# Turned attention weights sent from SBUF to SBUF in 16 transfers per pair of heads, their buffers doubled, and the projection weights placed where expert parameters come later

## The chip, the cores and the metric

One core of one Trainium2 chip runs the whole layer in one launch. The metric is the device time of one execution in microseconds (us), the median over runs. The profile is of one other execution of the same program; its times are read within that execution.

## The reference

The input is x, 8 batches of 512 tokens of width 128, float32. Two blocks follow each other, each with a layer norm ahead and a residual around it:

```
q, k, v = split_heads(ln(x) @ Wq), ...          # 16 heads of 64
scores  = q @ k^T + bias(rel_bias)              # 32 buckets of relative position
x       = x + (softmax(scores) @ v merged) @ Wo
h       = ln(x)
logits  = -|h - keys|^2 + h @ rw^T + rb          # 16 experts
w, e    = softmax(top4(logits))
x       = x + sum_k w_k * (gelu(h @ w1[e_k]^T + b1[e_k]) @ w2[e_k]^T + b2[e_k])
```

## The kernel before

**Attention.** The outer loop runs over the 8 batches b, the inner one over 8 pairs of heads i (`run_steps`); n = 8b + i numbers the pairs, 0 to 63. A step of TensorE computes the scores of its pair in four row tiles v (L1334) for the two heads hh, projects v, q and k for the next pair (L1285 to L1287), and finishes the pair before: it turns the probabilities of the row tiles v = 2, 3 with TensorE (`weights_t`, L1348) and multiplies them by the values in `weigh_late` (L1387); `weigh_early` (L1403) does the same for the row tiles v = 0, 1 and is the last thing in the step. The product with Wo follows a step later (`project_out`, L1414). All is float32; the projections and scores are made of three products of high and low parts.

Between score and product, VectorE adds the bias and finds the row maximum (L1040), ScalarE takes the exponential (L884), VectorE the reciprocal of the sum (L1046), and GpSimd divides (L816).

**How the row tiles v = 0, 1 are turned.** `turn_blocks` (VectorE, L1062) transposes blocks of 32 x 32 of `prob` into `turned`, two transposes for each v; they are counted in `tr_rdy`, four to a pair. The blocks then still have to move across groups of 32 partitions, which VectorE can't do. SP does it in `turn_weights`: for each v it stores `turned` into `pt_dram` in four transfers of 32 partitions each (128 KB, L678), and once all have landed loads the v half of `pt_d` from there in one transfer of 512 KB (L686). There is one `turned` and one `pt_d`. VectorE may write `turned[:, v]` for a pair only when the stores of the pair before have landed (`pt_wr[v]`), and SP may load `pt_d` only when `weigh_early` of the pair before is done (`c_rdy`). `weigh_early` waits for `pt_rd`. The very first pair and the last one (63) go by TensorE transposes and VectorE copies instead.

**SP's order.** SP issues everything in the order in which it is written in `step(b, i)`: `turn_weights` of the pair, at times the load of a batch of x, then expert parameters. Each expert is two transfers (`load_expert`, 514 KB and 64 KB, L655 and L656) into `params`, which overlaps the front of `shared` (AHEAD columns that nothing else uses) and then the bias `strips`, which come free pair by pair in the last batch. Five experts are loaded in batches 1 to 5, the other eleven in the last batch, the last two of them (`last_experts`) between the two halves of the stores of pair 62. `first_rows` fetches the first three blocks of gathered rows (`xb`, L734) between the two loads of that pair.

**Expert blocks.** After attention 79 blocks of 256 gathered rows follow, each for one expert: rows turned (L1469), hidden layer (L1481 to L1483), GELU (L916), second layer (L1494), result scattered (L851). In the last attention step, and in `drain`, the first blocks are interleaved with the end of attention: `turn(0, 0)` stands directly ahead of `weigh_early` of pair 62 on TensorE.

**Memory.** `w_hi`, `w_lo` (high and low parts of the three projection weights) belong to attention; `xb`, the gathered rows, takes memory that attention has given up, so `first_rows` waits for the last projection.

Of the kernel before, what the change touches and what calls it, by code (L numbers as in the profile page):

```python
# [20 lines left out]
F32 = mybir.dt.float32  # L21
# [8 lines left out]
P = 128  # L30
DH = 64
# [6 lines left out]
def layer_kernel(nc, x, wq, wk, wv, wo, rel_bias, onehot, ident, expert_no, before_tok, region, home_row, pad,  # L38
# [47 lines left out]
    with ExitStack() as ctx:  # L86
# [79 lines left out]
        turned = sb("turned", [P, 2, TC, TC, 2, BK], stack=attn)  # L166
        pt_d = sb("pt_d", [P, 2, TC, TC, 2, BK], stack=attn)
# [4 lines left out]
        stage = [turned[:, n].rearrange("p k j h r -> p (k j h r)") for n in range(2)]  # L172
        stage.append(pt_e[:].rearrange("p h j q -> p (h j q)")[:, 0:H * DH])
        scratch = shared[:, AHEAD + H * STRIP:]
# [7 lines left out]
        pt_dram = nc.dram_tensor("pt_dram", [2, 2, P, TC, TC * 2 * BK], F32, kind="Internal").ap()  # L182
# [24 lines left out]
        tr_rdy, pt_wr, pt_rd = sem("tr_rdy"), [sem(f"pt_wr{v}") for v in range(2)], [sem(f"pt_rd{v}") for v in range(2)]  # L207
# [14 lines left out]
        attn.close()  # L222

        xbt_hi = sb("xbt_hi", [P, 2, BLK], F32R)
# [3 lines left out]
        xb = sb("xb", [P, UN, BC, D + 1])  # L228
        home = sb("home", [P, UN, BC], I32)
        act_h = sb("act_h", [P, 2, FC, BLK])  # L230
# [6 lines left out]
        yk = shared[:, NE * EW:NE * EW + YB * TOP * S].rearrange("p (a k c d) -> p a k c d", k=TOP, c=TC, d=D)  # L237
# [19 lines left out]
        FIRST, OTHERS = slice(0, VW), slice(VW, H * DH)  # L257
# [380 lines left out]
        def _(sp):  # L638
# [31 lines left out]
            def turn_weights(b, i):  # L670

                n = b * NPR + i
                for v in range(2):
                    sp.wait_ge(tr_rdy, 4 * n + 2 * v + 2)
                    if n >= 3:
                        sp.wait_ge(pt_rd[v], 16 * (n - 2))
# [3 lines left out]
                    if v == 0 and (b, i) == (LAST, NPR - 2):  # L680
                        last_experts()
# [1008 lines left out]
```

## Time and profile before

| | us |
|---|---|
| median of 3 runs | 1121.62 (1121.6 to 1124.82) |
| profiled execution, first to last instruction | 1087.2 |
| TensorE busy | 1056.9 (97%) |
| VectorE busy | 834.8 (77%) |
| ScalarE busy | 839.7 (77%) |
| GpSimd busy | 685.9 (63%) |

The DMA engines moved 189.09 MB, and HBM was read for 101.18 MB and written for 88.23 MB. The attention steps last to about 765 us, the expert blocks from about 787 us to the end. A time is in microseconds from the first instruction; "busy" of TensorE counts matmuls, whose ends are modelled. In a row of the waits, the engine and line that waited stand ahead of the arrow, and what it waited for behind it. The hardware queue of SP is called SPq, its rows are the issues of transfers; when a transfer lands is another matter, told by the chain of waits or by the section on DMA.

### The profile page before, as it was taken

How to read it: one execution, taken by the hardware profiler on the slowest of the kernel's cores; microseconds unless marked ns; L12 is line 12 of the kernel's file. 1: busy time of each engine (PE TensorE's matmuls, PEld its weight loads, DVE VectorE, ACT ScalarE, POOL GpSimd, SP SyncE). 2: the span in 40 equal slices, each digit the busy share in tenths (PEclk: the TensorE clock that was granted, in tenths of full speed). 3: DMA queues.
4: the chain of work that ended last, by engine and by line, in shares of the span. 5: the costliest groups of instructions: out<-in, count | busy, mean ns of one | idle time of the engine just before them, and what ended most of it. 6: DMA issues, size and time to landing. Idle time of an engine off the chain costs nothing.

```text
span 1087.2 us, 27487 instructions
## 1 busy us (share of the span) xinstructions
PE 1056.9 (97%) x8509; PEld 863.7 (79%) x8510; DVE 834.8 (77%) x2568; ACT 839.7 (77%) x2050; POOL 685.9 (63%) x890
## 2 busy tenths in 40 slices
PE   8999999999999999999999999999799999999993
PEld 4777777777777777777777777777599999999993
DVE  6877888888888978988898888888546444457775
ACT  5888888888888888888888888878667666777661
POOL 4654556774776568477657756665756777655553
PEclk9999999999999999999999999999999999999997
DMA  7676666776676677576757666787722623234552
GB/s 212 177 198 192 194 172 181 206 210 171 207 208 184 179 198 208 165 222 194 201 163 216 194 174 194 207 261 227 252 66 82 158 70 105 79 95 133 162 174 69
DMA packets 135344, 189.09 MB, mean 174 GB/s; under 512 B 19000, under 2 KB 108608, under 8 KB 135216
## 3 DMA queue, kind: packets, MB, share of 16 engines
q1 hardware_dynamic: 126064, 170.65, 55.5%
q0 software_dynamic: 9152, 16.88, 4.6%
q8 instruction: 63, 1.03, 0.4%
q14 instruction: 65, 0.53, 0.2%
HBM read 101.18 MB, written 88.23 MB: 174 GB/s over the span
## 4 chain that ended last, share of the span: by engine, by line
PE 80%; DMA 6%; DVE 5%; issue 4%; POOL 2%; SPq 1%; ACT 1%; DVEq 0%; POOLq 0%; ACTq 0%
PE bank L1334 14%; PE bank L1494 13%; PE bank L1403 9%; PE bank L1348 8%; PE bank L1387 8%; PE bank L1414 4%; PE bank L1481 3%; PE bank L1483 3%; PE bank L1482 3%; PE bank L1285 3%; PE bank L1287 3%; PE bank L1286 3%; DMA pt_d<-pt_dram 3%; DVE shared L1040 2%; DMA pt_dram<-turned 2%
## 5 line engine op out<-in xcount | busy, mean ns | idle before, releaser
L816 POOL TENSOR_SCALAR shared<-shared,rinv 128x512 f32<-128x512 f32 x512 | 351.8, 699 | 224.9 <-DVE rinv L1046 222.9
L884 ACT ACTIVATE shared<-shared,nmax 128x512 f32<-128x512 f32 x512 | 368.4, 733 | 75.8 <-DVE nmax L1040 75.8
L1040 DVE CUSTOM_DVE_ANT_0 shared<-bank,shared 128x512 f32<-128x512 f32 x512 | 330.1, 682 | 77.6 <-issue 33.1
L851 POOL DMA_INDIRECT y_dram<-yb,home x158 | 162.0, 1026 | 94.0 <-issue 47.6
L372 POOL DMA_INDIRECT xs_dram<-copies,slot x128 | 134.8, 1053 | 62.0 <-issue 48.9
L1062 DVE STREAM_TRANSPOSE turned<-shared 128x512 f32<-128x512 f32 x248 | 161.0, 687 | 10.7 <-issue 10.7
L890 ACT ACTIVATE pt_e<-bank 128x512 f32<-128x512 f32 x256 | 145.1, 596 | 18.0 <-PE bank L1348 17.2
L1494 PE MATMUL bank<-shared,act_h 128*128 x1264 | 154.1, 275 | 1.3 <-DVE yb L1188 0.7
L1494 PEld LDWEIGHTS bank<-shared,act_h 128*128 128x128 f32 x1264 | 148.0, 192 | 1.9 <-issue 1.9
L1348 PE MATMUL bank<-idn,shared 128*128 128x128 f32 x1024 | 136.6, 276 | 0.5 <-DVE nmax L1040 0.5
L1348 PEld LDWEIGHTS bank<-idn,shared 128*128 128x128 f32 x1024 | 112.8, 141 | 24.1 <-issue 12.7
L1387 PE MATMUL bank<-pt_e,v_sb 128*64 128x256 f32 x1024 | 124.6, 385 | 3.5 <-DVE nmax L1040 3.0
L916 ACT ACTIVATE act_h<-bank,shared 128x256 f32<-128x256 f32 x316 | 124.2, 476 | 3.4 <-PE bank L1483 3.2
L1403 PE MATMUL bank<-pt_d,v_sb 128*64 128x256 f32 x1008 | 122.7, 385 | 3.8 <-DMA pt_d<-pt_dram 3.5
L1387 PEld LDWEIGHTS bank<-pt_e,v_sb 128*64 128x64 f32 x1024 | 71.1, 136 | 49.2 <-issue 23.6
L1334 PE MATMUL bank<-k_hi,q_lo 64*128 64x512 f32 x512 | 109.1, 421 | 0.9 <-DVE q_lo L1023 0.6
L884 ACT ACTIVATION_READ_ACCUMULATOR shared<-shared,nmax 128x1 f32 x512 | 106.6, 208 | 0.0
L1403 PEld LDWEIGHTS bank<-pt_d,v_sb 128*64 128x64 f32 x1008 | 73.6, 138 | 38.3 <-issue 7.9
L1334 PE MATMUL bank<-k_hi,q_hi 64*128 64x512 f32 x512 | 101.0, 388 | 0.0
L1334 PE MATMUL bank<-k_lo,q_hi 64*128 64x512 f32 x512 | 100.9, 388 | 0.0
L1481 PE MATMUL bank<-xbt_hi,w_lo 128*128 128x256 f32 x316 | 95.6, 303 | 0.0
L1188 DVE TENSOR_TENSOR yb<-bank,shared 128x256 f32<-128x256 f32 x79 | 33.5, 424 | 79.9 <-PE bank L1494 79.9
(162 smaller groups left out, 1886.7 us busy)
## 6 DMA issues: line engine op xcount, KB each, us to landing
pt_dram<-turned SPq DMA_DIRECT2D x496, 128.0 KB
pt_d<-pt_dram SPq DMA_DIRECT2D x124, 512.0 KB
xb<-xs_dram SPq DMA_DIRECT2D x79, 129.0 KB, 2.9
shared<-in_experts SPq DMA_DIRECT2D x16, 514.0 KB
shared<-y_dram SPq DMA_DIRECT2D x32, 256.0 KB, 4.6
shared<-roll_dram SPq DMA_DIRECT2D x4, 768.0 KB, 8.2
y_dram<-yb,home POOLq DMA_INDIRECT x158
xs_dram<-pad_sb SPq DMA_DIRECT2D x17, 129.0 KB, 2.2
```

The lines of the kernel that those rows point to most:

```text
L372: pool.indirect_dma_start(xs_dram, bass.IndirectOffsetOnAxis(ap=slot[:, c * TOP + k:c * TOP + k + 1], axis=0), copies[:, c, k % 2, :], Non ...
L816: pool.tensor_scalar(tile, tile, rinv[:, 2 * v + hh:2 * v + hh + 1], 1.0, ALU.mult, ALU.mult)\
L851: pool.indirect_dma_start(y_dram, bass.IndirectOffsetOnAxis(ap=home[:, j, c:c + 1], axis=0), yb[:, j, c, :], None, bounds_check=last_row, ...
L884: act.activation(prob[:, v, hh, :], prob[:, v, hh, :], ACT.Exp, bias=nmax[:, n:n + 1], scale=-1.0, accum_out=rsum[:, n:n + 1]).then_inc(ex ...
L890: act.activation(pt_e[:, hh, :, (v - 2) * P:(v - 1) * P], weights_bank(b, i, v, hh)[:].rearrange("p (j q) -> p j q", j=TC), ACT.Copy)\
L1040: dve.tensor_tensor_reduce(prob[:, v, hh, :], score_bank(v, hh)[:], strips[:, 2 * i + hh, v * P:v * P + S], -1.0, BIG, ALU.add, ALU.min, n ...
L1062: dve.transpose(turned[:, v, :, :, hh, :].rearrange("p k j r -> p j k r"), prob[:, v, hh, :].rearrange("p (j k c) -> p j k c", k=TC, c=BK) ...
L1334: mm = pe.matmul(score_bank(v, hh)[:], q[rows, i % 2, v * P:(v + 1) * P], k[rows, i % 2, :], start=(m == 0), stop=(m == 2))
L1348: mm = pe.transpose(weights_bank(b, i, v, hh)[:, j * P:(j + 1) * P], prob[:, v, hh, j * P:(j + 1) * P], idn[:])
L1387: pe.matmul(ps_a[DH * hh:DH * hh + DH, 2 * P:4 * P], v_sb[:, i // 2 % 2, j, col:col + DH], pt_e[:, hh, j, :], start=(j == 0), stop=(j == T ...
L1403: mm = pe.matmul(ps_a[DH * hh:DH * hh + DH, 0:2 * P], v_sb[:, i // 2 % 2, j, col:col + DH], src[:, :, :, j, hh, :].rearrange("p v a r -> p ...
L1494: mm = pe.matmul(ps_y[:, c * D:(c + 1) * D], act_h[:, q % 2, f, c * P:(c + 1) * P], params[:, bass.ds(w + (W2 + f * D), D)], start=(f == 0 ...
```

## The change

`turned` and `pt_d` get a second buffer each, chosen by the parity of the pair. `pt_dram` goes. SP waits for all four transposes of a pair and for `weigh_early` of two pairs before, and then issues 16 transfers, one for each group of 32 source partitions a and each group of 32 target partitions k: 32 partitions, two runs of 1 KB in each, 64 KB in all. They count up `pt_sent` of the parity, on which `weigh_early` waits; VectorE waits on it too, for the pair two before, ahead of the transposes.

To make room, the high and low projection weights become one tensor `weights`, laid out pair by pair at the front of the memory that `params` takes later, so that it comes free pair by pair in the last batch. `free_at(e, i)` says whether expert e fits into what is free after step i, and all 16 experts are loaded in the last batch, in the steps 0 to 6: experts 0; 6, 7; 1, 8; 2, 9, 10; 11, 12; 3, 13; 4, 5, 14, 15. Those of step 6 are issued ahead of `turn_weights` of pair 62, and `first_rows` behind it. `xb` gets memory of its own for the whole kernel.

```diff
@@ -139,39 +139,40 @@
+        xb = sb("xb", [P, UN, BC, D + 1])
 
 
         PROBS = 2 * TC * S
-        AHEAD = max(0, NE * EW - (H - 2) * STRIP)
-        shared = sb("shared", [P, AHEAD + H * STRIP + PROBS])
-        strips = shared[:, AHEAD:AHEAD + H * STRIP].rearrange("p (h m) -> p h m", h=H)
-        prob = shared[:, AHEAD + H * STRIP:].rearrange("p (c h s) -> p c h s", c=TC, h=2)
-        params = shared[:, 0:NE * EW]
+        AHEAD = NPR * 6 * P
+        assert NE * EW <= AHEAD + (H - 2) * STRIP
+        low = ctx.enter_context(ExitStack())
+        weights = sb("weights", [P, NPR, 3, 2, P], F32R, low)
+        shared = sb("shared", [P, H * STRIP + PROBS], stack=low)
+        strips = shared[:, 0:H * STRIP].rearrange("p (h m) -> p h m", h=H)
+        prob = shared[:, H * STRIP:].rearrange("p (c h s) -> p c h s", c=TC, h=2)
...
-        w_hi = [sb(f"w{n}_hi", [P, H * DH], F32R, attn)[:] for n in "kqv"]
-        w_lo = [sb(f"w{n}_lo", [P, H * DH], F32R, attn)[:] for n in "kqv"]
...
+        pt_d = sb("pt_d", [P, 2, 2, TC, TC, 2, BK], stack=attn)
...
-        turned = sb("turned", [P, 2, TC, TC, 2, BK], stack=attn)
-        pt_d = sb("pt_d", [P, 2, TC, TC, 2, BK], stack=attn)
+        turned = sb("turned", [P, 2, 2, TC, TC, 2, BK], stack=attn)
...
+        low.close()
+
+        late = sb("late", [P, AHEAD + H * STRIP + PROBS])
+        params = late[:, 0:NE * EW]
...
+        FIRST, OTHERS = slice(0, 2), slice(2, NPR)
+        PIECES = TC * TC * 16
+
+        def sent_by(n):
+
+            return PIECES * ((n + 1) // 2)
...
             def turn_weights(b, i):
 
                 n = b * NPR + i
-                for v in range(2):
-                    sp.wait_ge(tr_rdy, 4 * n + 2 * v + 2)
-                    if n >= 3:
-                        sp.wait_ge(pt_rd[v], 16 * (n - 2))
-                    for a in range(TC):
-                        sp.dma_start(pt_dram[n % 2, v].rearrange("(k c) a e -> a c k e", k=TC)[a],
-                                     turned[a * BK:(a + 1) * BK, v].rearrange("c k j h r -> c k (j h r)")).then_inc(pt_wr[v], 16)
-                    if v == 0 and (b, i) == (LAST, NPR - 2):
-                        last_experts()
-                if n:
-                    sp.wait_ge(c_rdy, n)
-                for v in range(2):
-                    sp.wait_ge(pt_wr[v], 64 * n)
-                    sp.dma_start(pt_d[:, v].rearrange("p a j h r -> p (a j h r)"),
-                                 pt_dram[n % 2, v].rearrange("p a e -> p (a e)")).then_inc(pt_rd[v], 16)
-                    if v == 0 and (b, i) == (LAST, NPR - 2):
-                        first_rows()
-
-            def free_to(b, i):
-
-                return AHEAD if b < LAST else AHEAD + 2 * STRIP * (i + 1)
-
-            loaded = [0]
-
-            def last_experts():
-
-                sp.wait_ge(neg_rdy, LAST * CHUNKS + (NPR - 1) * TILES)
-                while loaded[0] < NE:
-                    load_expert(loaded[0])
-                    loaded[0] += 1
+                par = n % 2
+                sp.wait_ge(tr_rdy, 4 * n + 4)
+                if n >= 2:
+                    sp.wait_ge(c_rdy, n - 1)
+                for a in range(TC):
+                    for k in range(TC):
+                        sp.dma_start(pt_d[k * BK:(k + 1) * BK, par, :, a].rearrange("c v j h r -> c v (j h r)"),
+                                     turned[a * BK:(a + 1) * BK, par, :, k].rearrange("c v j h r -> c v (j h r)"))\
+                            .then_inc(pt_sent[par], 16)
+
+            def free_at(e, i):
+
+                first, end = e * EW, (e + 1) * EW
+                used_up = (i + 2) // 2 * 2 * 6 * P + i % 2 * 4 * P
+                return (first >= AHEAD or min(end, AHEAD) <= used_up) and (end <= AHEAD or end <= AHEAD + 2 * STRIP * (i + 1))
+
+            def experts_of(i):
+
+                return [e for e in range(NE) if free_at(e, i) and not (i and free_at(e, i - 1))]
+
+            def load_experts(i):
+
+                sp.wait_ge(k_rdy, LAST * NPR + min(i + 2, NPR))
+                sp.wait_ge(neg_rdy, LAST * CHUNKS + (i + 1) * TILES)
+                for e in experts_of(i):
+                    load_expert(e)
 
             def load_table():
 
...
             def step(b, i):
+                if (b, i) == (LAST, NPR - 2):
+                    load_experts(i)
                 if (b, i) not in ((0, 0), (LAST, NPR - 1)):
                     turn_weights(b, i)
+                if (b, i) == (LAST, NPR - 2):
+                    first_rows()
                 n = b * NPR + i + 1
                 if 2 <= n < NB:
                     sp.dma_start(x_all[:, n * TC:(n + 1) * TC, :],
                                  x[n * S:(n + 1) * S].rearrange("(n p) d -> p n d", p=P)).then_inc(ld_x, 16)
-                if b == LAST:
-                    sp.wait_ge(neg_rdy, LAST * CHUNKS + (i + 1) * TILES)
-                for _ in range(2 if b == LAST else 1 if 1 <= b < 6 and i == 6 else 0):
-                    if loaded[0] < NE and (loaded[0] + 1) * EW <= free_to(b, i):
-                        load_expert(loaded[0])
-                        loaded[0] += 1
+                if b == LAST and i < NPR - 2:
+                    load_experts(i)
 
             run_steps(step, lambda: None)
-            assert loaded[0] == NE
+            assert sum(len(experts_of(i)) for i in range(NPR - 1)) == NE
             run_blocks(sp, block_rows, lambda: None, LEAD - 1, rows, row_at, rest, looped=FETCH_FROM // UN)
             for n in range(LATE_STORES, NB):
                 store(n)
...
                 if (b, i) == (0, 0):
                     copy_first(v)
                     return
-                if later_turn(b, i):
-                    dve.wait_ge(pt_wr[v], 64 * (b * NPR + i - 1))
+                n = b * NPR + i
+                if n > 2:
+                    dve.wait_ge(pt_sent[n % 2], sent_by(n - 2))
                 for hh in range(2):
                     dve.wait_ge(norm_rdy, b * CHUNKS + TILES * i + 2 * v + hh + 1)
                     if hh == 0:
                         dve.nop(nofuse=True)
-                    dve.transpose(turned[:, v, :, :, hh, :].rearrange("p k j r -> p j k r"),
+                    dve.transpose(turned[:, n % 2, v, :, :, hh, :].rearrange("p k j r -> p j k r"),
                                   prob[:, v, hh, :].rearrange("p (j k c) -> p j k c", k=TC, c=BK)).then_inc(tr_rdy, 1)
 
             def copy_early(v):
 
                 n = LAST * NPR + NPR - 1
-                dve.wait_ge(pt_wr[v], 64 * (n - 1))
+                dve.wait_ge(pt_sent[n % 2], sent_by(n - 2))
                 for hh in range(2):
                     dve.wait_ge(early_rdy, 2 * v + hh + 1)
                     if hh == 0:
                         dve.nop(nofuse=True)
-                    dve.tensor_copy(turned[:, v, :, :, hh, :].rearrange("p a j r -> p j a r"),
+                    dve.tensor_copy(turned[:, n % 2, v, :, :, hh, :].rearrange("p a j r -> p j a r"),
                                     early_bank(v, hh)[:].rearrange("p (j a r) -> p j a r", j=TC, a=TC)).then_inc(tr_rdy, 1)
 
             def copy_first(v):
...
                 n = b * NPR + i
                 last = n == NB * NPR - 1
                 src = turned if last else pt_d
+                par = n % 2
                 if last or n == 0:
                     pe.wait_ge(tr_rdy, 4 * (n + 1))
                 else:
-                    for v in range(2):
-                        pe.wait_ge(pt_rd[v], 16 * n)
+                    pe.wait_ge(pt_sent[par], sent_by(n))
                 for j in range(TC):
                     for hh in range(2):
                         col = (i % 2) * P + DH * hh
                         mm = pe.matmul(ps_a[DH * hh:DH * hh + DH, 0:2 * P], v_sb[:, i // 2 % 2, j, col:col + DH],
-                                       src[:, :, :, j, hh, :].rearrange("p v a r -> p (v a) r"),
+                                       src[:, par, :, :, j, hh, :].rearrange("p v a r -> p (v a) r"),
                                        start=(j == 0), stop=(j == TC - 1))
                 mm.then_inc(c_rdy, 1)
 
```

The engines' code for the projections and for `weights_hi` and `weights_lo` names the same columns in `weights`, and `copy_early` and `copy_first` name the buffer of their parity.

## Rows read from the trace of the kernel before

**Rows 1.** The page, busy time of each engine, share of the span, instructions.

```profile
PE 1056.9 (97%) x8509; PEld 863.7 (79%) x8510; DVE 834.8 (77%) x2568; ACT 839.7 (77%) x2050; POOL 685.9 (63%) x890
```

**Rows 2.** Windows: length, busy time of each engine, granted clock, DMA share, GB/s.

```profile
95.00:760.00 665.00, 662.15 (x5263) 504.83 (x5260) 571.30 (x1811) 552.62 (x1350) 429.40 (x588) 1.00 0.69 197
760.00:800.00 40.00, 33.80 (x261) 26.15 (x261) 17.80 (x49) 25.77 (x63) 26.68 (x34) 0.96 0.56 187
```

**Rows 3.** Waits of TensorE before `weigh_early`: total us, times, longest us.

```profile
PE bank L1403 <- DMA pt_d<-pt_dram: 3.5, 5, 1.7
PEld bank L1403 <- issue: 7.9, 12, 2.0
```

**Rows 4.** Timeline of VectorE, the later transposes of pairs 16, 19 and 21.

```profile
213.93 1.29 DVE L1062 STREAM_TRANSPOSE turned<-shared 128x512 f32<-128x512 f32 x2
...
247.99 0.70 DVE L1062 STREAM_TRANSPOSE turned<-shared 128x512 f32<-128x512 f32 x1
...
274.57 0.71 DVE L1062 STREAM_TRANSPOSE turned<-shared 128x512 f32<-128x512 f32 x1 [1.22 <-issue]
```

**Rows 5.** Timeline of TensorE, the first `weigh_early` matmuls of the same three pairs.

```profile
224.52 0.39 PE L1403 MATMUL bank<-pt_d,v_sb 128*64 128x256 f32 x2
...
261.31 0.44 PE L1403 MATMUL bank<-pt_d,v_sb 128*64 128x256 f32 x2
...
285.13 0.44 PE L1403 MATMUL bank<-pt_d,v_sb 128*64 128x256 f32 x2
```

**Rows 6.** Chain of waits from 570 to 586 (pair 46): start, us, what.

```profile
575.02 0.44 SPq L678
575.46 0.04 issue
575.50 2.54 DMA pt_dram<-turned
...
578.05 6.64 DMA pt_d<-pt_dram
584.69 0.14 issue
```

**Rows 7.** Timeline of SP's queue, two bursts of four issues.

```profile
215.25 1.75 SPq L678 DMA_DIRECT2D pt_dram<-turned  x4
...
429.93 2.15 SPq L678 DMA_DIRECT2D pt_dram<-turned  x4
```

**Rows 8.** The page's DMA issues: the one store of 64 KB, us to landing.

```profile
roll_dram<-shared SPq DMA_DIRECT2D x1, 64.0 KB, 1.9
```

**Rows 9.** Windows with columns as in rows 2: four stores, and the junction's start.

```profile
215.90:217.90 2.00, 2.00 (x19) 1.40 (x16) 1.97 (x7) 1.24 (x3) 1.83 (x3) 1.00 0.84 214
...
764.00:774.00 10.00, 9.05 (x78) 7.17 (x79) 7.80 (x24) 6.65 (x18) 8.58 (x11) 1.00 0.91 320
```

**Rows 10.** DMA queue of instructions: packets, MB, share; whole span, and 429.7 to 431.2.

```profile
q8 instruction: 63, 1.03, 0.4%
...
q8 instruction: 1, 0.02, 4.1%
```

**Rows 11.** All issues of line 678: duration ns min/median/max, first and last start.

```profile
L678 SPq DMA_DIRECT2D pt_dram<-turned x496: 302/436/1745, 32.0 to 771.6; - x166
```

**Rows 12.** Timeline of SP's queue at the junction.

```profile
767.13 0.82 SPq L656 DMA_DIRECT2D shared<-in_b  x1
...
772.26 0.96 SPq L686 DMA_DIRECT2D pt_d<-pt_dram  x1
774.42 1.55 SPq L734 DMA_DIRECT2D xb<-xs_dram  x3
778.95 0.33 SPq L686 DMA_DIRECT2D pt_d<-pt_dram  x1
```

**Rows 13.** Timeline of TensorE at the junction.

```profile
780.91 0.41 PE L1469 MATMUL bank<-idn,xb 128*128 128x128 f32 x2 [0.91 <-DMA xb<-xs_dram]
783.06 3.63 PE L1403 MATMUL bank<-pt_d,v_sb 128*64 128x256 f32 x16 [1.74 <-DMA pt_d<-pt_dram]
```

More of the change, by code:

```diff
@@ L165, in layer_kernel @@
         rinv = sb("rinv", [P, TILES], stack=attn)
-        turned = sb("turned", [P, 2, TC, TC, 2, BK], stack=attn)
-        pt_d = sb("pt_d", [P, 2, TC, TC, 2, BK], stack=attn)
+        turned = sb("turned", [P, 2, 2, TC, TC, 2, BK], stack=attn)
         pt_e = sb("pt_e", [P, 2, TC, 2 * P], stack=attn)
         ctxt = sb("ctxt", [P, S], stack=attn)
-        stage = [turned[:, n].rearrange("p k j h r -> p (k j h r)") for n in range(2)]
+        stage = [turned[:, 0, n].rearrange("p k j h r -> p (k j h r)") for n in range(2)]
         stage.append(pt_e[:].rearrange("p h j q -> p (h j q)")[:, 0:H * DH])
-        scratch = shared[:, AHEAD + H * STRIP:]
+        scratch = shared[:, H * STRIP:]
         onehot_sb = scratch[0:NBUCKET, 0:ROLL].rearrange("p (a m) -> p a m", a=2)
@@ L206, in layer_kernel @@
         early_rdy, first_rdy = sem("early_rdy"), sem("first_rdy")
-        tr_rdy, pt_wr, pt_rd = sem("tr_rdy"), [sem(f"pt_wr{v}") for v in range(2)], [sem(f"pt_rd{v}") for v in range(2)]
+        tr_rdy, pt_sent = sem("tr_rdy"), [sem("pt_sent_even"), sem("pt_sent_odd")]
         c_rdy, c_cp, o_rdy, res_rdy = (sem(n) for n in ("c_rdy", "c_cp", "o_rdy", "res_rdy"))
@@ L234, in layer_kernel @@
         pad_at = sb("pad_at", [1, NE], I32)
-        yk = shared[:, NE * EW:NE * EW + YB * TOP * S].rearrange("p (a k c d) -> p a k c d", k=TOP, c=TC, d=D)
+        yk = late[:, NE * EW:NE * EW + YB * TOP * S].rearrange("p (a k c d) -> p a k c d", k=TOP, c=TC, d=D)
         ps_xt, ps_y, ps_h = banks[0], banks[1], (banks[2:4], banks[4:6])
@@ L984, in weights_hi @@
             def weights_hi(n, cols):
-                act.activation(w_hi[n][:, cols], stage[n][:, cols], ACT.Copy).then_inc(w_hi_rdy, 1)
+                act.activation(weights[:, cols, n, 0], stage[n].rearrange("p (i c) -> p i c", c=P)[:, cols], ACT.Copy).then_inc(w_hi_rdy, 1)
             act.wait_ge(ld_w[0], 16)
@@ L1106, in weights_lo @@
                 dve.wait_ge(w_hi_rdy, order)
-                dve.tensor_tensor(w_lo[n][:, cols], stage[n][:, cols], w_hi[n][:, cols].bitcast(F32), ALU.subtract)\
+                dve.tensor_tensor(weights[:, cols, n, 1], stage[n].rearrange("p (i c) -> p i c", c=P)[:, cols],
+                                  weights[:, cols, n, 0].bitcast(F32), ALU.subtract)\
                     .then_inc(w_lo_rdy, 1)
@@ L1289, in project_k @@
             def project_k(i, bank):
[L1291 to L1292 removed]
+                three(bank[:], weights[:, i, 0, 0], weights[:, i, 0, 1], xnt_hi[:], xnt_lo[:]).then_inc(k_rdy, 1)
             def project_q(i, bank):
[L1296 to L1297 removed]
+                three(bank[:], weights[:, i, 1, 0], weights[:, i, 1, 1], xnt_hi[:, ::-1], xnt_lo[:, ::-1]).then_inc(q_rdy, 1)
             def project_v(i, bank):
[L1301 removed]
+                pairs = slice(i // 2 * 2, i // 2 * 2 + 2)
                 for a in range(2):
@@ L1304, in project_v @@
                     tok = slice(c * P, (c + 1) * P)
-                    mm = three(bank[:, a * VW:(a + 1) * VW], xnt_hi[:, tok], xnt_lo[:, tok],
-                               w_hi[2][:, cols], w_lo[2][:, cols])
+                    mm = three(bank[:, a * VW:(a + 1) * VW].rearrange("p (i c) -> p i c", c=P), xnt_hi[:, tok], xnt_lo[:, tok],
+                               weights[:, pairs, 2, 0], weights[:, pairs, 2, 1])
                 mm.then_inc(v_rdy, 1)
```

14 lines of the change are left out of this document (2 added, 12 removed).

## The prediction

> **What bounds the kernel now.** I read the page's busy line first [rows 1]: TensorE is busy for 1056.9 of 1087.2 us, so only about 30 us can be won from waits. The windows say where they lie [rows 2]: in the attention steps between 95 and 760 us TensorE is busy for 662.15 of 665 us, so 2.85 us are idle; in the 40 us in which attention gives way to the expert blocks 6.2 us are idle, and the mean clock is 0.96, which costs 40 x 0.04 = 1.6 us more. The waits name what I can win [rows 3]: `weigh_early` (L1403) waited 3.5 us for the transfer into `pt_d`, in five places, and its weight loads 7.9 us in twelve (these views count the same waits twice and include start-up of the pipeline). The other 30-odd us are the start, the tail and the junction's waits for VectorE, which the change doesn't touch.
>
> So the question is narrow: when do the turned weights of a pair arrive, against the time at which TensorE comes to them? Call A the time from the end of a pair's last transpose to the start of its `weigh_early` in an undelayed step. Pair 16: 213.93 + 1.29 = 215.22 to 224.52, A = 9.30. With the same 1.29 for two transposes, pair 21 has 275.86 to 285.13, A = 9.27, and pair 19 has 249.28 to 261.31, A = 12.0 [rows 4, 5]. A depends on the place in a batch of eight pairs. Pairs 21 and 19 are the ends of the eight; read the same way, places 0, 4 and 5 lie at 9.30, 9.5 and 9.27, places 1, 6 and 7 at about 9.9, places 2 and 3 at 11 and 12.
>
> Before, the way goes through DRAM [rows 6]: the last of four stores starts at 575.50 and is seen done 2.54 us later, the read that follows lands after another 6.64 us, TensorE starts 0.14 us after that. This pair (46) was late by some 0.4 to 0.8 us. An ordinary pair arrives 1 to 2 us early: margins are thin already.
>
> **The change, part by part.** The eight stores and two loads of a pair become 16 SBUF-to-SBUF transfers of 64 KB, issued only when all four transposes are done.
>
> Call R the time from the last transpose to data ready. Issue: four back-to-back issues take 1.75 us [rows 7], and one of them repeats every 0.44 + 0.04 = 0.48 us [rows 6], so the first takes 1.75 - 3 x 0.48 + 0.04 = 0.35. The last of 16 thus starts 0.02 + 0.35 + 14 x 0.48 = 7.1 us after the transpose. I assume that the issue costs the same for a quarter of a store's pieces; no row shows a form like it. Landing of the last: no row shows an SBUF-to-SBUF transfer. The nearest are the one 64 KB store out of SBUF, 1.9 us [rows 8], and the last store of a burst of four with the others queued before it, 2.54. Below these it may lie, since nothing goes to DRAM and nothing is queued: in 215.9 to 217.9 the four stores flow at 214 GB/s [rows 9], at which 64 KB take 0.31 us, less than the 0.48 between issues, so no backlog forms. I take 1.8, nearest to the 1.9 row, with 1.2 and 2.54 as ends. R = 7.1 + 1.8 + 0.14 = 9.0; ends 8.4 and 9.8.
>
> At 9.0 no place waits. But the chain of 16 issues is exposed to disturbances. Instruction packets of 16 KB (63 in 1087 us, one in 17 us) pass through the same DMA engines, and the burst beside one took 2.15 instead of 1.75 us [rows 7, 10]; the longest single issue is 1.745 against 0.436 [rows 11]. Issue and landing last 9 us, so about half of the pairs meet one; I take +0.7 us, between 0.4 and the 1.3 of the longest. Then R = 9.7 and places 5, 0 and 4 wait 0.45, 0.40 and 0.2. A wait at one pair is slack for the next, which hardly matters here. Sum: 1.05 a batch, x 0.5, x 62 / 8 = 4 us added. Against this stand the waits of before between 95 and 760, which go whole: -3 us.
>
> The doubled buffers: SP's new wait for `c_rdy` is for `weigh_early` two pairs back (done by 1.9 us after its start, a step before), and VectorE's for `pt_sent` of two pairs back, 23 us old at the transpose. Both are over long before, so nothing queued behind them on SP (the load of `x_all`, the experts) or on VectorE is held. DRAM loses 124 MB of traffic (62 pairs, 1 MB each way); nothing in attention waits for bandwidth. The layout of `weights` and the own place of `xb` cost nothing: the same instructions with other strides, on ScalarE and VectorE, which are not late, and `first_rows` keeps its waits.
>
> Expert parameters: all 16 now come in the last batch (before, 11), by `free_at` in steps 0 to 6: 1, 2, 2, 3, 2, 2, 4. Each is two issues, 0.95 us of SP. In step 3 that is 2.9 us after 7.6 us of turning, 10.5 of an 11.5 us step: it fits.
>
> The junction: before, SP issued two experts between the two halves of pair 62's stores, the first load of `pt_d` at 772.26 (0.96 us), the first rows of `xb` at 774.42, and the second load only at 778.95, when the stores had landed behind the experts [rows 12]. TensorE turned `xb` at 780.91 and started `weigh_early` at 783.06, 1.74 us idle, then at half clock [rows 13]. After: SP is through with pair 61 and its two experts at about 766, four experts take 8 x 0.48 = 3.8, to 770; 16 transfers take 7.6, to 777.6; their data stand behind some 3.5 MB of experts, which at the 320 GB/s of this stretch [rows 9] need 11 us and are gone by 776, so they land at 779.5. `first_rows` comes last: 1.2 us of register loads as between 773.2 and 774.4, issue at 779, landing 2.1 to 2.9 us later, 781.5. `turn(0, 0)` stands ahead of `weigh_early` on TensorE, so this starts at 781.6 to 782 instead of 783.06: -1.5 us at most, +1.5 if the queue of experts holds SP back (such issues took up to 0.8 us [rows 12]). I take -1.
>
> Sum: -3 + 4 - 1 = 0, rounded to -1 for the gain at the junction's clock, of which 1.6 us is the bound. The profiled execution would go from 1087.2 to about 1086; the median of the runs shown is 1121.6, 34.4 above that span, and none of this lies in the edits. So 1120.5.
>
> A rule against the change: the Trainium skill, "DMA: Bandwidth & Descriptors", section "Rules for kernel authors", says to coalesce many small transfers, since under 64 KB one pays mostly overhead. The traces hold overheads apart from each other: four issues in 1.75 us, landing 2.54 us after the last. By the rule's section on one DMA, a fixed 2.0 us each, 16 in a row would be an estimated 32 us a pair; by that row they overlap, and only the last one's counts.
>
> **The rivals.**
> 1. Faster. The last transfer lands in 1.2 us, R = 8.4, 9.1 with a disturbance: no place ever waits. -3, the junction at -3 because the rows come sooner too, and its 1.6 us of clock: -7.6, 1114. For it: SBUF is both ends, no backlog. Against it: the 1.9 us row.
> 2. Slower: the issue chain takes the place of the round trip. From R = 9.27 on, undisturbed pairs wait. With 2.54 for the landing R = 9.8: places 4, 5 and 0 wait 0.3, 0.25 and 0.5, 1.0 a batch; disturbed (10.5) the places 4, 5, 6, 7, 0 wait 1.0, 0.25, 0.4, 0.15, 1.0, 2.8 in all. The mean 1.9 x 62 / 8 = 15 us, -3 and -1: +11, 1132. For it: every 0.1 us of the issue interval is 1.4 us of R.
> 3. The transfers don't flow. 32 partitions give 214 GB/s where four stores do it together [rows 9]; if an SBUF-to-SBUF piece goes at half of that, it takes 0.61 us, 16 x 0.61 + 1.6 = 11.4: waits of 1.9, 0.25, 1.3, 0.2, 1.9 and 0.4 in places 4 to 7, 0 and 2 (each wait takes something off the next), 5.9 a batch, 46 us; net +42, 1163. The Trainium skill ("SBUF — State Buffer", "Door 1: The DMA port swizzle") says that 32 partitions reach 8 of the 16 ports, an estimated 218 GB/s of its 436; the row's 214 agrees for stores. Against the rival: reads and writes have never shared a burst here.
>
> **How the numbers follow.** Forecast 0.42, rival 1 0.27, rival 2 0.25, rival 3 0.06. A difference under 0.3% (3.4 us) can't be told from none; the forecast's own range is 1117.5 to 1124.5, the other cases lie outside. So faster 0.27, same 0.42, slower 0.31. The range takes in rivals 1 and 2 with some way beyond the second's 1132, and leaves out rival 3 and the far ends: 1113 to 1138.
>
> **What would show it.** In the profile after: the first to the last of 16 issues 7.1 us, more in about half of the pairs; the last one landing 1.2 to 2.5 us on; waits of `weigh_early` of about 4 us in places 0, 4 and 5 of the batches, none in 2 and 3; SP's issues of experts at 766 to 770 and `weigh_early` of pair 62 near 782. The prediction is wrong if an issue of this form takes other than 0.44 us, if waits appear in places 2 and 3 (rival 3), or if SP stops between issues because the DMA engines are full.

## The result and the profile after

The changed kernel is slower: 1226.2 us median against 1121.61 us, ratio 1.0911 (95% interval 1.0885 to 1.0937). The experiments below ran later, on three chips, on which the kernel before took 1087.54, 1088.25 and 1088.15 us; once more there, the changed kernel has 1193.17 against 1088.25 us, ratio 1.098 (1.0939 to 1.1022). So both kernels were some 33 us quicker than in the first comparison, and the loss in microseconds is the same, 104.6 and 104.9. Each ratio is to the kernel before on the same chip.

The page of the first profile after, busy time as in [rows 1] and the HBM line; then the waits, columns as in [rows 3]:

```profile
PE 1104.1 (90%) x8509; PEld 879.7 (72%) x8510; DVE 830.6 (68%) x2568; ACT 839.8 (69%) x2050; POOL 692.5 (57%) x890
...
HBM read 36.16 MB, written 23.22 MB: 49 GB/s over the span
```

```profile
PEld bank L1403 <- DMA pt_d<-turned: 83.9, 40, 4.0
...
PE bank L1403 <- DMA pt_d<-turned: 69.7, 36, 3.5
```

TensorE, 97% busy before, is busy for 90% of a span of 1223.8 us. `weigh_early` (L1403) waits 69.7 us for the transfers where it waited 3.5 us. The DRAM traffic is gone as intended, and it gained nothing.

Why it waits is seen in one pair. The chain of waits of the changed kernel, pair 22, columns as in [rows 6]; 11 of the 16 issues are left out, and the last one is the start of the row of the DMA:

```profile
319.79 1.22 DVE turned L1066 x2
321.01 0.02 issue
321.02 0.59 SPq L686
321.61 0.04 issue
321.65 0.60 SPq L686
...
324.86 1.10 SPq L686
...
330.47 0.60 SPq L686
331.07 0.04 issue
331.11 2.06 DMA pt_d<-turned
333.18 0.04 issue
333.22 1.95 PE bank L1403 x16
```

An issue repeats every 0.60 + 0.04 = 0.64 us, not every 0.48 as those of [rows 6]. The last of 16 starts at 331.11, 10.1 us after the transposes (9.6 us had none been held up; one took 1.10 us). It has landed 2.06 us later, and TensorE starts at 333.22: R = 12.2 us, above every A of [rows 4, 5]. All issues of the form, columns as in [rows 11]:

```profile
L686 SPq DMA_DIRECT2D pt_d<-turned x992: 585/597/1917, 37.3 to 879.3; - x199
```

The median is 597 ns against 436 for the stores, and the shortest, 585 ns, is close to it: no issue of this form is cheap. The long ones have company: each of the 36 issues above 0.9 us overlaps one of the 62 packets of 16 KB of instructions, as in [rows 10], while only 66 of all 992 issues do.

### The profile page after: what moved, and what is told of

It reads as the page before. It is cut to its first block, busy times and chain, and to the rows that moved or that the text cites. A ratio compares the mean times of both kernels' runs of the same rounds, so it can differ in the third digit from the quotient of the medians.

```text
span 1223.8 us, 27682 instructions
## 1 busy us (share of the span) xinstructions
PE 1104.1 (90%) x8509; PEld 879.7 (72%) x8510; DVE 830.6 (68%) x2568; ACT 839.8 (69%) x2050; POOL 692.5 (57%) x890
## 4 chain that ended last, share of the span: by engine, by line
PE 37%; SPq 25%; DVE 17%; issue 7%; DMA 7%; ACT 3%; POOL 2%; another core or an unknown queue 0%; ACTq 0%; DVEq 0%; POOLq 0%
SPq L686 24%; PE bank L1494 13%; PE bank L1403 7%; DVE shared L1043 6%; PE bank L1334 6%; DMA pt_d<-turned 5%; DVE turned L1066 4%; PE bank L1483 3%; PE bank L1481 2%; PE bank L1482 2%; DVE q_lo L1026 1%; POOL shared L819 1%; DVE k_lo L1021 1%; PE bank L1469 1%; PE bank L1348 1%
## 5 line engine op out<-in xcount | busy, mean ns | idle before, releaser
L854 POOL DMA_INDIRECT y_dram<-yb,home x158 | 169.8, 1075 | 128.6 <-issue 81.7
L1403 PE MATMUL bank<-pt_d,v_sb 128*64 128x256 f32 x1008 | 145.9, 440 | 69.7 <-DMA pt_d<-turned 69.7
L1494 PE MATMUL bank<-late,act_h 128*128 x1264 | 161.9, 283 | 10.8 <-ACT act_h L919 5.7
L1403 PEld LDWEIGHTS bank<-pt_d,v_sb 128*64 128x64 f32 x1008 | 78.5, 156 | 123.0 <-DMA pt_d<-turned 83.9
L1494 PEld LDWEIGHTS bank<-late,act_h 128*128 128x128 f32 x1264 | 151.9, 196 | 17.6 <-issue 17.4
L919 ACT ACTIVATE act_h<-bank,late 128x256 f32<-128x256 f32 x316 | 125.4, 480 | 42.4 <-remote 22.5
L900 ACT ACTIVATE ctxt<-bank 128x512 f32<-128x512 f32 x64 | 38.4, 600 | 134.6 <-PE bank L1403 124.2
L1190 DVE TENSOR_TENSOR yb<-bank,late 128x256 f32<-128x256 f32 x79 | 33.5, 424 | 111.5 <-PE bank L1494 83.2
```

Of the source, the lines that this page charges most:

```text
L854: pool.indirect_dma_start(y_dram, bass.IndirectOffsetOnAxis(ap=home[:, j, c:c + 1], axis=0), yb[:, j, c, :], None, bounds_check=last_row, ...
L1403: mm = pe.matmul(ps_a[DH * hh:DH * hh + DH, 0:2 * P], v_sb[:, i // 2 % 2, j, col:col + DH], src[:, par, :, :, j, hh, :].rearrange("p v a r ...
L1494: mm = pe.matmul(ps_y[:, c * D:(c + 1) * D], act_h[:, q % 2, f, c * P:(c + 1) * P], params[:, bass.ds(w + (W2 + f * D), D)], start=(f == 0 ...
```

## The experiments

Theory A: SP's chain of issues, 16 at 0.64 us behind the last transpose, makes the weights late; the stalls, and half clock behind them, are the loss. Rival B: the rest of the change (memory layout, experts in the last batch, `first_rows` behind everything) costs a good part. Rival C: the transfers' data flow is slow between 32 partitions, not their issue. The expectations of the first four runs count absolute times from the 1121.6 us of the first comparison; what compares is the ratio.

### The kernel before and the kernel after, once more

> The kernel before, once more, for its span and the way its time is spread. The profiled execution of before had a span of 1087.2 us beside a median of 1121.6, that of the changed kernel 1223.8 beside 1226.2. If the profiled execution of before was merely a quick one, this one's span lies near 1119 us and the 32 us more lie in the expert blocks (blocks of 3.5 to 4 us instead of 3.44), not in attention, whose steps stay at 11.5 to 13.2 us.

Measured: 1086.39 us, ratio 0.9997 (0.9981 to 1.0013), span 1085.9. The profile of before shown above, with its span of 1087.2, is like the executions here and unlike the 1121.6 us beside it; the span near 1119 did not come. The medians on the three chips lie within 0.8 us of each other, so the first comparison's 1121.6 stands alone; whether its chip or something else of that occasion made it so, no run shows.

> The changed kernel once more, beside the kernel before on this chip, for a comparison inside one chip of attention (95 to 750 us) and the expert blocks. Theory A: a ratio of 1.085 to 1.095 to before; all of it in attention and at the junction, 85 to 100 us: 60 to 70 us of waits of weigh_early and 1.7 us for each stretch of half clock that follows one; the expert blocks as before within 3 us. Rival B': part of the loss lies in the expert blocks (the first profile of after had 35 us more there than that of before), because something of the change slows them: then 20 us or more in the blocks here too.

Measured: 1193.17 us, ratio 1.098, span 1189.0; ratio and loss are a little above what I expected. Windows, columns as in [rows 2], from the first instruction to the start of `weigh_early` of pair 62, so that both hold the same work, and from there to the end: first of before, then of after.

```profile
0.00:782.90 782.90, 770.01 (x6036) 582.02 (x6038) 660.66 (x2073) 643.96 (x1568) 492.79 (x699) 1.00 0.70 200
782.90:1085.90 303.00, 284.62 (x2474) 280.86 (x2474) 174.61 (x496) 194.88 (x482) 190.81 (x192) 0.98 0.37 108
```

```profile
0.00:885.40 885.40, 798.91 (x6035) 589.89 (x6036) 660.15 (x2071) 643.83 (x1567) 499.91 (x707) 0.96 0.43 103
885.40:1189.00 303.60, 286.07 (x2475) 281.23 (x2474) 174.87 (x497) 194.87 (x483) 184.30 (x184) 0.97 0.38 109
```

Nearly all of the loss lies ahead of that point: 885.4 against 782.9, 102.5 us more. The expert blocks take 303.6 against 303.0, so rival B' falls. The 102.5 us split into two terms. TensorE's idle time grew from 12.9 (782.9 - 770.01) to 86.5 us (885.4 - 798.91), by 73.6 us. Its busy time, for the same matmuls, grew by 28.9 us, since the mean clock fell from 1.00 to 0.96. The trace has 16 stretches of half clock in attention, 58.0 us together, and a 17th that begins at the junction; half of the 58.0 is 29. Here is one of them at the `weigh_early` of pair 20, first TensorE's row in the timeline, with its wait in brackets, then the window of that stretch, where the clock is 0.50:

```profile
302.79 3.56 PE L1403 MATMUL bank<-pt_d,v_sb 128*64 128x256 f32 x16 [2.89 <-DMA pt_d<-turned]
...
302.70:306.10 3.40, 3.31 (x16) 1.71 (x16) 0.39 (x5) 0.00 (x0) 3.36 (x6) 0.50 0.36 85
```

Behind a stall of 2.89 us the 16 matmuls take 3.56 us, against 1.95 at full clock (pair 22 above). The matmuls of line 1403 have 23.4 of the 28.9 us.

The first profile of after has the same attention: `weigh_early` of pair 62 starts at 884.1 there. Its expert blocks, though, take 339.7 us, 36 more than here, so for the changed kernel the difference between the two occasions lies in the expert blocks.

### The way through DRAM put back, all else kept

```diff
                 par = n % 2
-                sp.wait_ge(tr_rdy, 4 * n + 4)
+                store_half(0)
+                store_half(1)
                 if n >= 2:
                     sp.wait_ge(c_rdy, n - 1)
-                for a in range(TC):
-                    for k in range(TC):
-                        sp.dma_start(pt_d[k * BK:(k + 1) * BK, par, :, a].rearrange("c v j h r -> c v (j h r)"),
-                                     turned[a * BK:(a + 1) * BK, par, :, k].rearrange("c v j h r -> c v (j h r)"))\
-                            .then_inc(pt_sent[par], 16)
+                load_half(0)
+                load_half(1)
```

`store_half(v)` holds the four stores and `load_half(v)` the one load of before, with `pt_dram`, `turned` and `pt_d` by parity.

> The changed kernel with the old way through DRAM put back (eight stores, two loads), and everything else of the change kept: doubled buffers, weights under the expert parameters, all 16 experts in the last batch, own memory for xb, first_rows last. Theory A (SP's chain of 16 issues at 0.64 us each is what costs): the time is that of before within 0.5%, 1116 to 1127 us, and weigh_early waits under 5 us between 95 and 760. Rival B (memory layout, late experts or the place of first_rows cost a good part): over 1140 us. Rival C (the transfers' own flow costs, not their issue): as A.

Measured: 1092.89 us, ratio 1.0042 (1.0015 to 1.007). Waits of TensorE:

```profile
PE bank L1484 <- DMA xb<-xs_dram: 4.7, 1, 4.7
PE bank L1418 <- DMA pt_d<-pt_dram: 3.3, 3, 2.5
```

With this one part undone, 9.4 of the 9.8% are gone (1.098 to 1.0042). Rival B holds only the rest, 0.4%, of which the wait for the first rows of `xb` (L1484) at the junction is the largest piece.

### Shape and count of the transfers

Rival C, and the question what makes an issue dear, need other shapes. The first kernel puts v next to the run, so that a transfer moves one run of 2 KB a partition:

```diff
-        pt_d = sb("pt_d", [P, 2, 2, TC, TC, 2, BK], stack=attn)
+        pt_d = sb("pt_d", [P, 2, TC, 2, TC, 2, BK], stack=attn)
...
-                        sp.dma_start(pt_d[k * BK:(k + 1) * BK, par, :, a].rearrange("c v j h r -> c v (j h r)"),
-                                     turned[a * BK:(a + 1) * BK, par, :, k].rearrange("c v j h r -> c v (j h r)"))\
+                        sp.dma_start(pt_d[k * BK:(k + 1) * BK, par, a].rearrange("c v j h r -> c (v j h r)"),
+                                     turned[a * BK:(a + 1) * BK, par, k].rearrange("c v j h r -> c (v j h r)"))\
```

> The changed kernel with both buffers laid out so that the two row tiles v lie side by side: each of the 16 transfers moves one run of 2 KB for each of 32 partitions instead of two of 1 KB. Same bytes, same count. If an issue's 0.60 us come from the shape (two runs, three dimensions), it falls to 0.44 or less, R to about 9.2 us and the time to 1118 to 1135. If they come with every transfer between two places in SBUF, the issue stays at 0.60 and the time at 1220 to 1230. Rival C (flow) expects 1220 to 1230 as well.

The other three send the same 1 MB in 8, 12 and 16 transfers of all 128 partitions. In them nothing moves across partitions, so this part of the computation is left out; they show the time of the transfers and no result:

```diff
-                for a in range(TC):
-                    for k in range(TC):
-                        sp.dma_start(pt_d[k * BK:(k + 1) * BK, par, :, a].rearrange("c v j h r -> c v (j h r)"),
-                                     turned[a * BK:(a + 1) * BK, par, :, k].rearrange("c v j h r -> c v (j h r)"))\
+                for v in range(2):
+                    for a in range(TC):
+                        for q in range(2):
+                            js = slice(2 * q, 2 * q + 2)
+                            sp.dma_start(pt_d[:, par, v, a, js].rearrange("c j h r -> c (j h r)"),
+                                         turned[:, par, v, a, js].rearrange("c j h r -> c (j h r)"))\
```

This is the one with 16. The one with 8 has no loop over q and sends all of j at once; the one with 12 does that for v = 0 alone and keeps the two pieces for v = 1.

> The changed kernel with eight transfers of 128 partitions, one run of 1 KB each, in place of 16 of 32 partitions; the same 1 MB is sent, but nothing moves across partitions, so this part of the computation is left out. Theory A: the last issue starts 7 x 0.64 = 4.5 us (or 3.4 at 0.48) after the last transpose, R is 6.5 us or less, weigh_early never waits, the time is that of before less 3 to 8 us, 1112 to 1122. Rival B: stays over 1200. Rival C: if 1 MB needs its 10 us between two places in SBUF whatever the shape, R stays near 12 and the time near 1225.

> As the kernel with eight transfers of 128 partitions (nothing moves across partitions, so this part of the computation is left out), but the four pieces of v = 1 are cut in two: twelve transfers, the same 1 MB. Theory A: each issue 0.64 us, the last starts 7.6 to 7.7 us after the last of v = 1 is ready, R is 7.7 + 1.7 + 0.4 = 9.8 us, at the margins of 9.3 to 12. Waits of 0.5 us in places 0, 4 and 5 and more where an issue is held up: 1 to 2.5% above the kernel with eight, 1090 to 1108 us. If the loss came from the 32-partition pattern and not from the count of issues, this one is as quick as with eight (1084).

> As the kernels with eight and twelve transfers of 128 partitions (nothing moves across partitions, this part of the computation is left out), with all eight pieces cut in two: 16 transfers of 64 KB, 1 MB. Theory A (the count of issues, at 0.64 us each, whatever the shape): as the changed kernel, ratio 1.08 to 1.10, R 11.7 us. If 32 partitions against 128 matter beyond the issue (the flow through fewer ports), it stays clearly quicker than the changed kernel, 1.02 to 1.06.

The issues of the four kernels, duration in ns (min/median/max), in this order: one run; 8, 12 and 16 of 128 partitions:

```profile
L686 SPq DMA_DIRECT2D pt_d<-turned x992: 507/591/2187, 36.2 to 866.4; - x199
```

```profile
L686 SPq DMA_DIRECT2D pt_d<-turned x496: 464/601/2122, 36.4 to 771.7; - x166
```

```profile
L688 SPq DMA_DIRECT2D pt_d<-turned x744: 464/601/1817, 38.5 to 785.4; - x186
```

```profile
L688 SPq DMA_DIRECT2D pt_d<-turned x992: 464/601/2055, 38.6 to 882.2; - x199
```

| kernel | transfers of | ratio (95%) | waits of `weigh_early` (PE row) |
|---|---|---|---|
| changed | 16 x 64 KB, 32 partitions, 2 runs | 1.0980 (1.0939 to 1.1022) | 71.1 us |
| one run | 16 x 64 KB, 32 partitions, 1 run | 1.0875 (1.0833 to 1.0917) | 65.8 us |
| 16 whole | 16 x 64 KB, 128 partitions | 1.0903 (1.0853 to 1.0953) | 69.0 us |
| 12 whole | 4 x 128 and 8 x 64 KB, 128 partitions | 1.0070 (1.0043 to 1.0098) | 5.7 us |
| 8 whole | 8 x 128 KB, 128 partitions | 0.9969 (0.9951 to 0.9986) | none |

The waits of the kernel with 12 and of that with 16:

```profile
PE bank L1405 <- DMA pt_d<-turned: 5.7, 9, 1.3
```

```profile
PE bank L1405 <- DMA pt_d<-turned: 69.0, 40, 3.6
```

The median issue takes 0.59 to 0.60 us in every one of these shapes; the minima belong to the first issue of a burst, which takes 0.46 to 0.51 us in these four kernels and 0.585 in the changed one. An issue of 128 KB takes as long as one of 64 KB, so it is not the bytes. 32 or 128 partitions make no difference to the time (the second and the third row lie within each other's intervals), so rival C falls. The count does: with 8 issues the last starts 4.4 us after the transposes and nobody waits; with 12 it starts at 7.1 and the data come at the margins; with 16 it starts at 10 and they come behind them. Eight, twelve and sixteen came out as expected. The kernel with one run per partition did not get its cheap issue; it is 1% quicker than the changed one, with a cheaper first issue, 591 against 597 ns for the others, and 5.0 instead of 8.5 us of wait for `xb`. Why an issue between two places in SBUF takes 0.16 us more than one with DRAM at one end was not found; none of the shapes tried changes it.

The kernel with 8 also prices all that was to be won. With no wait at all for these weights, the kernel gains 0.31%, 3.4 us. It has the same experts and `first_rows` in the same places as the changed kernel, and TensorE waits only 1.0 us for `xb`.

### Four of the sixteen issued by ScalarE

```diff
-                for a in range(TC):
+                for a in range(TC - 1):
...
+                if exists(one[0]) and one != (0, 0):
+                    n = b * NPR + i - 1
+                    a, par = TC - 1, n % 2
+                    act.wait_ge(tr_rdy, 4 * n + 4)
+                    if n >= 2:
+                        act.wait_ge(c_rdy, n - 1)
+                    for k in range(TC):
+                        act.dma_start(pt_d[k * BK:(k + 1) * BK, par, :, a].rearrange("c v j h r -> c v (j h r)"),
+                                      turned[a * BK:(a + 1) * BK, par, :, k].rearrange("c v j h r -> c v (j h r)"))\
+                            .then_inc(pt_sent[par], 16)
```

> The changed kernel with the last four of the 16 transfers issued by ScalarE, at the start of the next step behind its copy of the context, the twelve others by SP. Theory A, if each queue takes its own 0.64 us: SP's last issue starts 7.7 us after the transpose, R falls from 11.7 to 9.8, and the time to 1.01 to 1.04 of before; ScalarE pays 4 x 0.64 = 2.6 us a step and is then busy for 11.4 of 11.5 us, which may cost some of it. If both queues share one maker of descriptors, the issues lengthen to 1.2 us while both are at it and the time stays at 1.08 or more.

Measured: 1130.67 us, ratio 1.0402 (1.0378 to 1.0425), at the upper end of what I expected. The two queues' issues, and what TensorE waited for between 95 and 750 us:

```profile
L686 SPq DMA_DIRECT2D pt_d<-turned x744: 585/597/2036, 38.4 to 817.6; - x186
L944 ACTq DMA_DIRECT2D pt_d<-turned x248: 592/622/1348, 38.7 to 808.9; - x124
```

```profile
PE bank L1358 <- DVE nmax L1053: 17.7, 37, 1.1
PE bank L1413 <- DMA pt_d<-turned: 0.8, 3, 0.3
```

Both queues issue at once at nearly their own pace (0.597 and 0.622 us; 244 of ScalarE's 248 issues overlap one of SP's), so an issue occupies its queue and not a maker that all share. The wait for the transfers is all but gone (0.8 us), and more than half of the loss with it (1.098 to 1.040). Half clock is gone too: in the whole profile L1358 waits 44 times, never above 1.5 us, and no stretch of half clock falls into attention. A price on ScalarE is left: four issues are 2.5 us of a step in which its exponentials wait, and with them VectorE's maxima and TensorE's next transposes (L1358). That was foreseen as a possibility. Up to `weigh_early` of pair 62 the kernel takes 41.9 us more than before; 21.3 of these are idle time of TensorE. In the other 20.6 us it is counted as busy at full clock with the same matmuls, 11 of them in the transposes of L1358. Whether that is waiting too, no view shows.

### TensorE kept at work while it waits

```diff
+                if 0 < n < NB * NPR - 1:
+                    for _ in range(16):
+                        pe.matmul(ps_a[:, 0:2 * P], ones_bf[:], ones_bf[:].unsqueeze(1).broadcast_to([P, 2, P]), start=True, stop=True)
```

> The changed kernel with 16 matmuls more (bf16 ones, 128x256, results overwritten) ahead of weigh_early's wait in pairs 1 to 62, so that TensorE does 1.7 us of work of no use where it otherwise stands still. If the 17 stretches of half clock in attention come from standing still, they go or nearly so, the granted clock of attention rises from 0.96 to 0.99 or more, and up to 34 us come back, less what the matmuls cost in the steps without a wait, about 30 x 1.7 = 50 us: ratio 1.07 to 1.11. If the half clock has another cause, the clock stays at 0.96 and the ratio is 1.10 to 1.15.

Measured: 1206.76 us, ratio 1.1091 (1.1068 to 1.1113). Window of attention:

```profile
95.00:885.00 790.00, 789.10 (x6324) 597.06 (x6323) 587.92 (x1857) 569.17 (x1392) 442.49 (x607) 1.00 0.41 96
```

The mean clock is 1.00 where it was 0.96, and between 95 and 885 us no stretch of half clock is left. So the half clock is a consequence of TensorE's standing still and not a cost of its own: 28.9 of the 102.5 us hang on the 73.6. Buying it back this way costs more than it gives, since the added matmuls also stand in the steps that had no wait. They take 120.0 us up to `weigh_early` of pair 62, more than the 102.5 that were to be had, and that point comes at 902.8 instead of 885.4 us.

### The way through DRAM with the doubled buffers put to use

```diff
                 store_half(0)
+                load_half(0)
+                if (b, i) == (LAST, NPR - 2):
+                    first_rows()
                 store_half(1)
-                load_half(0)
                 load_half(1)
```

Besides, experts 4 and 5 go ahead of pair 62, and 14 and 15 behind its first stores.

> The way through DRAM with the doubled buffers put to use: SP loads the v = 0 half of pt_d before it stores the v = 1 half, so that only 512 KB are left to load at the end, and at the junction experts 4 and 5 go ahead of pair 62, experts 14 and 15 behind its first stores, and the first rows of xb ahead of its second stores. Expected: data ready 1.5 us or more earlier than before (R 7 to 7.5 instead of 8.5 us), no wait of weigh_early between 95 and 760 (3 to 6 us in before), the junction no later than before: ratio 0.992 to 0.998. If SP's wait for the first stores to land holds up the later stores instead, the ratio is 1.00 or more.

Measured: 1114.73 us, ratio 1.025 (1.0228 to 1.0272): a miss, on the side that the expectation names last. `weigh_early` waits 25.6 us in all. The chain of waits of one pair (16):

```profile
212.23 0.30 SPq L689
...
213.52 4.47 DMA pt_dram<-turned
...
218.06 0.34 SPq L694
...
218.50 0.38 SPq L689
...
219.88 3.92 DMA pt_dram<-turned
223.80 0.02 issue
223.82 4.18 DMA pt_d<-pt_dram
```

The first stores start on time, 0.02 us behind their transposes, and the last of them takes 4.47 us to land; the second ones, which need nothing but transposes that ended at 217.34, are queued behind that wait and start at 218.50. SP waiting for a landing holds up whatever stands behind it, and it stands in such waits for 192.3 + 164.6 us in this kernel (its two longest rows), against 104.6 in before. With doubled buffers the order of before, both stores and then both loads, is the better one (1.0042 against 1.025, though the junction differs too); with single buffers the other order wasn't tried.

### The junction alone

The kernel with the way through DRAM put back, and the order of before at the junction:

```diff
                 store_half(0)
+                if at_end:
+                    load_expert(NE - 2)
+                    load_expert(NE - 1)
                 store_half(1)
...
                 load_half(0)
+                if at_end:
+                    first_rows()
                 load_half(1)
```

> The kernel with the way through DRAM put back (1.0042 of before, where TensorE waited 4.7 us for the first rows of xb), and the junction put back too: experts 4 and 5 ahead of pair 62, 14 and 15 between its two stores, first_rows between its two loads. If the place of first_rows behind four experts and all transfers was what that kernel still lost, the ratio is 0.998 to 1.001 and TensorE waits under 2 us for xb; if the late experts themselves cost it, 1.003 to 1.005 stays.

Measured: 1092.15 us, ratio 1.0034 (1.0023 to 1.0045), and TensorE still waits for the rows of `xb`:

```profile
PE bank L1491 <- DMA xb<-xs_dram: 3.6, 1, 3.6
```

So the place of `first_rows` does not cost the rest, and the first of my two explanations of it was wrong. The late experts are left: four are due in step 6, ahead of or among the transfers of pair 62, where before there were two. That they cost the 0.3 to 0.4% is argued by exclusion and not shown, and if they do, it is only together with the way through DRAM: the kernel with eight transfers has the same four, and waits 1.0 us for the rows.

## Why the prediction was wrong

**The step that failed: the duration of an issue.** I took 0.44 + 0.04 us from stores to DRAM and said that no row showed a form like the new one, but gave bounds only to the landing, none to the issue. It was 0.60 + 0.04. Over 14 intervals these 0.16 us are 2.2 us of R, and the first issue took 0.63 us with its gap where I had 0.35: 9.6 us to the start of the last issue where I had 7.1. The margins of 9.3 to 12 us that I had read [rows 4, 5] were right, and they made the number decisive; I even wrote that 0.1 us of the interval is 1.4 us of R, and then did not spend it on the range.

**What was right.** The landing: taken 1.8 + 0.14, measured 2.06 + 0.04 in the pair above. Disturbances of a single issue of 0.5 us and more, as the 1.10 there, which overlap packets of instructions. The absence of a flow limit: 16 transfers of 32 and of 128 partitions take the same time. (The 214 GB/s of [rows 9], which the prediction sets beside 8 ports, belong to four stores that together read all 128 partitions, so they say little of 32.) No wait of SP or VectorE for the doubled buffers. The other strides in the weights and `xb`'s own place cost nothing that shows. The Trainium skill's rule against small transfers ("DMA: Bandwidth & Descriptors", "Rules for kernel authors") gives the right sign for this change: here the overhead that counts is the 0.64 us of the queue for each transfer, not a fixed 2 us each, and 32 us a pair is not what came. The 2.0 us that the prediction took from the Trainium skill stand there for a transfer issued by GpSimd (same page, "Anatomy of one DMA — SWDGE (gpsimd) path"), and these are issued by SP.

**The sum by the right term.** With R = 9.6 + 2.1 = 11.7 the recursion of the prediction (a place waits R - A less the wait before it) gives 2.2, 0.2, 1.6, 0.2, 2.2, 0 and 0.7 us in places 4 to 7 and 0 to 2, 7.1 a batch, 55 us; with the 0.7 us of disturbance in half of the pairs 67. Measured in the second profile of after: `weigh_early` waits 71.1 us, and the growth of idle time is 73.6 us, junction included. The waits lie where the recursion puts them, with medians over the batches of 2.8, 1.4, 2.9 and 2.2 us in places 0, 2, 4 and 6 and of 0 in the odd places. So waits in place 2, which the prediction kept for rival 3, came from a longer issue alone. Rival 2 named this mechanism, the issue chain in place of the round trip, at a quarter of the chance and with R = 9.8; rival 3 had R = 11.4 for a cause that the kernels of 128 partitions exclude.

**The term that was missing in every case: the clock.** The prediction charged half clock only at the junction and put it at nothing in attention. 16 stretches of it there add 28.9 us, two fifths as much again as the idle time. Even with the right R the forecast would have been some 29 us short.

**The junction.** Taken as 1 us quicker. It was slower: TensorE waited 7.9 us for the first rows of `xb` in the first profile of the changed kernel, against the 0.91 us in [rows 13], as four experts and 16 transfers stand ahead of them on SP's queue. Its timeline in that profile:

```profile
863.34 0.77 SPq L662 DMA_DIRECT2D late<-in_experts  x1
...
869.06 10.81 SPq L686 DMA_DIRECT2D pt_d<-turned  x16
881.24 4.05 SPq L737 DMA_DIRECT2D xb<-xs_dram  x8
```

The 16 end at 879.9, and the rows go out 1.4 us later, as foreseen for the register loads. The four experts took 5.6 us to issue, not 3.8, and the 16 transfers 10.8, not 7.6.

## What to carry to other kernels

When a transfer is split, first price the issue on its queue in its own form, times the count, and set the sum against the margin at the consumer: here 16 x 0.64 us against 9.3 us decided everything, and bytes saved decided nothing. Ask before building what the whole wait is worth; a kernel that sends the same bytes in eight issues showed 0.3%. And where TensorE is the bound, a recurring stall can have a second price in the clock, here 28.9 us on 73.6; the shorter stalls with ScalarE's issues, up to 1.5 us, had none.

## What the runs showed of the hardware that I had not expected

- An issue from SP for a transfer between two places in SBUF takes 0.59 to 0.60 us (medians of 496 to 992 issues), whatever the shape tried; one from SBUF to DRAM takes 0.44 us. Issued from ScalarE it takes 0.62 us, also while SP issues.
- An issue of 0.6 us grows to 0.9 us and more nearly always beside a 16 KB packet of instructions: 36 of 36 such issues in the first profile of the changed kernel, 35 of 37 in the second.
- Stalls of TensorE of 2.1 us on average and 3.4 at most, every second step or so, brought 16 stretches of half clock, 1.2 instead of 2.4 GHz, 58.0 us together; with TensorE kept at work in them there were none in attention between 95 and 885 us.
- The same kernel took 1121.6 us on one occasion and 1087.5 to 1088.3 us on three chips later; the loss by the change was 104.6 and 104.9 us.
